# A cross-attention network on one core: layers unrolled, the next layer's keys and values inside a layer's last unit, normalisation through PSUM on ScalarE, MLP weight splits on ScalarE and VectorE

## What is computed

```python
# stage 0: grouped attention over the context, 32 heads of 16, 8 key heads, then residual and layer norm
x = layer_norm(x + softmax(q k^T / 4 + mask) v @ Wo + bo) * gamma + beta
# layers 0 and 1: cross attention, 16 heads of 128, one extra key and value (bias_k, bias_v) per head
for ly in (0, 1):
    h = layer_norm(x) * scale + offset
    x = x + softmax(concat(k, bias_k) . q / sqrt(128)) . concat(v, bias_v) @ wo + bo
# MLP of width 2048
h = layer_norm(x) * scale + offset
x = x + gelu(h @ w_fc1 + b_fc1) @ w_fc2 + b_fc2
```

## Time and profile before

| what | value |
|---|---|
| median of 3 runs | 2657.53 us (2656.21 to 2658.27) |
| profiled execution | 2658.52 us |
| its span, first to last instruction | 2656.7 us |
| mean granted clock of PE | 0.963 |
| PE busy | 2428.2 us, 91% |
| DVE, ACT, POOL busy | 1313.4, 791.8, 882.5 us |
| transfers | 120.09 MB, mean 45 GB/s |

### The profile page before, as it was taken

The page is one execution under the profiler, slowest core; times in us unless marked ns, Lnnn a source line. Parts: engine busy times, 40 slices in busy tenths (PEclk is TensorE's granted clock), DMA queues, the critical chain, the costliest instruction groups (busy, mean ns, idle before and its releaser), DMA issues.

```text
span 2656.7 us, 40799 instructions
## 1 busy us (share of the span) xinstructions
PE 2428.2 (91%) x14896; PEld 2076.7 (78%) x14896; DVE 1313.4 (49%) x2066; ACT 791.8 (30%) x2390; POOL 882.5 (33%) x568
## 2 busy tenths in 40 slices
PE   6867999998899999888977779999988999998888
PEld 5656888887788888667765568888877888886676
DVE  6976333344533343555479763334355334336444
ACT  5862222222222222211158522222222222222111
POOL 4853322232422232322157532223224223224221
PEclk9988999999999999999989889999999999999999
DMA  4001101010201010100130011011111011101000
GB/s 174 10 9 68 56 32 39 32 55 22 78 32 39 32 55 32 44 32 32 64 140 9 25 60 48 32 39 39 47 57 43 32 39 39 47 32 44 32 32 32
DMA packets 34534, 120.09 MB, mean 45 GB/s; under 512 B 3456, under 2 KB 3712, under 8 KB 33408
## 3 DMA queue, kind: packets, MB, share of 16 engines
q1 hardware_dynamic: 34432, 118.69, 12.7%
HBM read 114.48 MB, written 4.19 MB: 45 GB/s over the span
## 4 chain that ended last, share of the span: by engine, by line
PE 77%; DVE 8%; issue 6%; POOL 4%; ACT 3%; DMA 1%; SPq 0%; DVEq 0%; POOLq 0%; ACTq 0%
PE PS L453 64%; PE PS L664 4%; PE PS L646 4%; PE PS L655 2%; POOL X L319 1%; DVE X L1012 1%; DMA BO<-in_bo_rows 1%; PE PS L521 1%; PE PS L555 1%; DVE HF L1087 1%; DVE XN L988 1%; POOL W L306 1%; DVE BNS L1022 1%; DVE HB L1240 0%; DVE AT L1079 0%
## 5 line engine op out<-in xcount | busy, mean ns | idle before, releaser
L453 PE MATMUL PS<-AT,W 128*128 128x512 f32 x2496 | 609.2, 396 | 25.2 <-DVE HF L1087 12.1
L453 PEld LDWEIGHTS PS<-AT,W 128*128 128x128 f32 x2496 | 474.3, 191 | 129.9 <-issue 13.2
L1012 DVE TENSOR_TENSOR X<-PS,X 128x512 f32<-128x512 f32 x416 | 284.4, 690 | 333.1 <-PE PS L453 326.4
L394 POOL TENSOR_TENSOR PR<-PR,RC 128x512 f32<-128x512 f32 x128 | 133.5, 1043 | 932.1 <-DVE RC L1178 932.1
L453 PE MATMUL PS<-CT,W 128*128 128x512 f32 x1584 | 401.2, 403 | 28.8 <-DVE W L306 25.6
L453 PE MATMUL PS<-W,CT 128*128 128x256 f32 (+1 forms) x3264 | 410.3, 286 | 0.0
L453 PEld LDWEIGHTS PS<-W,CT 128*128 128x128 f32 x3264 | 399.6, 194 | 0.6
L453 PE MATMUL PS<-W,CX 128*128 128x512 f32 x1584 | 388.7, 399 | 11.8 <-DVE X L1012 8.6
L453 PEld LDWEIGHTS PS<-CT,W 128*128 128x128 f32 x1584 | 292.8, 192 | 86.7 <-DVE W L306 26.0
L453 PEld LDWEIGHTS PS<-W,CX 128*128 128x128 f32 x1584 | 292.9, 189 | 76.9 <-DVE X L1012 12.7
L313 POOL TENSOR_SCALAR W<-RAW 128x1024 fp32r<-128x1024 f32 (+1 forms) x136 | 154.6, 1137 | 546.5 <-PE PS L453 524.8
(11 more groups left out here) (102 smaller groups left out, 2531.9 us busy)
## 6 DMA issues: line engine op xcount, KB each, us to landing
RAW<-in_wq SPq DMA_DIRECT2D x44, 512.0 KB, 4.1
RAW<-in_wo SPq DMA_DIRECT2D x44, 512.0 KB, 3.3
RAW<-in_wk SPq DMA_DIRECT2D x40, 512.0 KB, 3.3
RAW<-in_wv SPq DMA_DIRECT2D x40, 512.0 KB, 3.3
X<-in_x SPq DMA_DIRECT2D x2, 2048.0 KB, 10.0
BVR<-in_bv_rows SPq DMA_DIRECT2D x8, 512.0 KB, 4.2
BIASVR<-in_biasv_rows SPq DMA_DIRECT2D x8, 512.0 KB, 5.6
out<-X SPq DMA_DIRECT2D x4, 1024.0 KB, 4.4
```

The lines of the kernel that those rows point to most:

```text
L394: nc.gpsimd.tensor_tensor(PR[:, :, 0:P], PR[:, :, 0:P], RC[:, 0, 0:BT].unsqueeze(2).to_broadcast([P, BT, P]), ALU.mult).then_inc(norm_done, 1)
L453: ins = nc.tensor.matmul(out, lhs(c, a), rhs(c, b), start=(k == 0), stop=(k == total - 1))
L1012: V_.tensor_tensor(X[:, tile, :], PS[:, bank, :], X[:, tile, :], ALU.add).then_inc(done, 1)
```

## The change

- The loop over the two layers is unrolled in the code of every engine (`for ly in range(LAYERS)`); the loop over `g` stays for the inner pairs.
- K has a buffer for each of the two heads.
- A layer's last unit is written out by hand. Towards layer 1 it holds keys and values of the next layer's first unit and the transposes of the normalised block 0; the rows of the last unit come as ordinary `rows`, and the next layer's first unit (`next_unit`) has no keys of its own. Towards the MLP it holds the transposes, parts of the last rows, and the first hidden block comes ahead of the rest of the last rows.
- Statistics are taken as rows are added (`add_block(..., measured=True)`).
- `to_at` is gone: ACT writes the scaled chunk as high part to AT and again, in place, to the PSUM bank; DVE subtracts from the bank (`lows`). `warm` is a one-element activation that loads a function table ahead of its use.
- In the MLP, PE's order is hidden m, down m-1 throughout, across pairs; ACT writes the high part of the slabs (`whi`), DVE the low part (`wlo`), POOL none but the first pair's v and o slabs.
- SP loads bias rows at two points inside the layer before; POOL subtracts and adds them inside the last and first units.

The diff, cut to its core:

```diff
-        K = in_arena("K", [P, BT, 132], F32, 2048)
+        K = in_arena("K", [P, 2, BT, 132], F32, 2048)
...
+                sp.wait_ge(v_ev, half_units(hf, 0) * 2 + NB1)
+                load_rows(1, 0)
+                with sp.Fori(G1 // 2 + 1, G1 + 1, 1) as g:
+                    load_slabs(g)
+                sp.wait_ge(v_ev, half_units(hf, 1) * 2)
+                load_rows(1, 1)
+                load_bo(2)
...
+                    even(G1 - 1)
+                    n = b0 + (NB1 - 1)
+                    weights(n, 0)
+                    if ly + 1 < LAYERS:
+                        sub_rows(ly + 1, 0)
+                    pool.wait_ge(q_ps, n * 2 + 2)
+                    psplit(0, lq + G1)
+                    if ly + 1 < LAYERS:
+                        psplit(2, lv + G1)
+                        weights(n, 1)
+                        add_layer_bo(ly + 1, 0)
+                        sub_rows(ly + 1, 1)
+                    else:
+                        weights(n, 1)
...
+                add_layer_bo(LAYERS, 0)
+                psplit(2, lv)
                 pool.wait_ge(o_ps, half_units(hf, LAYERS) * BT)
                 psplit(3, lq)
-                with pool.Fori(1, FG // 2, 1) as gp:
...
+                add_layer_bo(LAYERS, 1)
...
+                    def next_unit():
+                        queries(b0, 0, 0, lq, at_now)
+                        values(b0 + 1, 1, lv, -5, (0,))
+                        scores(b0, 0)
+                        queries(b0, 0, 1, lq)
+                        pe.wait_ge(q_ev, b0 * 2 + 2)
+                        pe.wait_ge(k_ev, b0 * 2 + 2)
+                        norm_t(norm_index(hf, ly), 1, BANKS_WARM)
+                        transposes(b0, 0)
+                        values(b0 + 1, 1, lv, -5, (1,))
+                        pe.wait_ge(at_lo, at_now + C + 1)
+                        weigh(b0, 0, 0)
+                        scores(b0, 1)
+                        pe.wait_ge(at_lo, at_now + 2 * C)
+                        keys(b0 + 1, 1, 0, lk)
+                        queries(b0 + 1, 1, 0, lq)
+                        transposes(b0, 1)
+                        values(b0 + 1, 1, lv, -5, (2, 3))
+                        weigh(b0, 0, 1)
+                    def last_unit_to_layer():
...
+                        scores(n, 1)
+                        keys(n + 1, 0, 0, lk + G1)
+                        values(n + 1, 0, lv + G1, -5, (0, 1))
+                        transposes(n, 1)
+                        pe.wait_ge(t_ev, n * 2 + 2)
+                        norm_t(norm_index(hf, ly + 1), 0, BANKS_NEXT)
+                        weigh(n, 1, 1)
+                        values(n + 1, 0, lv + G1, -5, (2, 3))
+                        rows(n, lq + g)
+                        keys(n + 1, 0, 1, lk + G1)
+                    def last_unit_to_mlp():
+                        g, n = G1 - 1, b0 + (NB1 - 1)
+                        scores(n, 0)
+                        keys(n, 1, 1, lk + g)
+                        rows(n - 1, lq + g)
+                        queries(n, 1, 1, lq + g)
+                        transposes(n, 0)
+                        scores(n, 1)
+                        weigh(n, 1, 0)
+                        norm_t(norm_index(hf, LAYERS), 0, BANKS_LAST, range(2))
+                        pe.wait_ge(cx_lo, n * 2 + 1)
+                        rows_part(0, 0)
+                        rows_part(1, 0)
+                        pe.wait_ge(exp_done, n * 2 + 2)
+                        norm_t(norm_index(hf, LAYERS), 0, BANKS_LAST, range(2, C))
+                        transposes(n, 1)
+                        weigh(n, 1, 1)
...
+                hidden(0, 0, True, (0,))
+                last_rows()
+                hidden(0, 0, True, (1,))
+                hidden(0, 1, True)
+                down(0, 0, True, range(2))
+                norm_t(norm_index(hf, LAYERS), 1, BANKS_MLP)
+                down(0, 0, True, range(2, BT))
+                down(0, 1, True)
+                hidden(0, 2, True)
+                hidden(0, 3, True)
+                down(0, 2, True)
+                with pe.Fori(1, FG // 2, 1) as gp:
+                    hidden(gp, 0)
+                    down(gp - 1, 3)
                     for m in range(1, 4):
+                        hidden(gp, m)
+                        down(gp, m - 1)
+                down(FG // 2 - 1, 3)
...
+                def norm_high(ly, tb, banks, chunks=range(C)):
+                    t, cols = norm_index(hf, ly) * TB + tb, layer_cols(ly)
+                    for c in chunks:
+                        act.wait_ge(tr_ps, t * C + (c + 1))
+                        for dst, done in ((AT[:, 0, c, tb * BTOK:(tb + 1) * BTOK], at_hi), (PS[:, banks[c], :], f_done)):
+                            nc.scalar.activation(dst, PS[:, banks[c], :], ACT.Identity, ...).then_inc(done, 1)
...
+                def whi(n, count, done):
+                    act.wait_ge(ld[n], count * 16 + 16)
+                    act.wait_ge(*done)
                     take_wait(act)
+                    nc.scalar.activation(W[:, n, 0, :], RAW[:, n, :], ACT.Copy).then_inc(w_hi[n], 1)
...
+                        if first and m == 0:
+                            root((hf + 1) * 8 - 1)
+                            warm(ACT.Gelu)
                         if first and m == 1:
+                            norm_high(LAYERS, 1, BANKS_MLP)
+                        if m < 2 and not first:
+                            whi(2 + m, (lv, lq)[m] + gp, (m_ps, m0 * BT - (1 - m) * BT))
+                        if m >= 2 and not last:
+                            whi(m - 2, (lq, lv)[m - 2] + gp + 1, (h_ps, m0 * 2 + 2 * m + 2))
...
+                def lows(i, tb, banks, chunks=range(C)):
+                    t = i * TB + tb
+                    for c in chunks:
+                        dve.wait_ge(f_done, t * C + (c + 1))
+                        V_.tensor_tensor(AT[:, 1, c, tb * BTOK:(tb + 1) * BTOK], PS[:, banks[c], :],
                                          AT[:, 0, c, tb * BTOK:(tb + 1) * BTOK].bitcast(F32), ALU.subtract).then_inc(at_lo, 1)
...
+                        add_block(n - 1, 0, True)
+                        cx_low(n, g, 0)
+                        top(n, 1)
+                        variances(rounds + 2, 1e-5)
+                        inverse(n, 1)
+                        roots(rounds + 2)
+                        dve.wait_ge(tr_ps, i * TB * C)
+                        apply(0)
+                        kev(n + 1, 0, 0, layer_cols(ly + 1))
+                        vev(n + 1, 0, 0, (0,), ly + 1)
+                        lows(i, 0, BANKS_NEXT, range(2))
+                        cx_low(n, g, 1)
+                        lows(i, 0, BANKS_NEXT, range(2, C))
+                        vev(n + 1, 0, 0, (1,))
...
+                def first_pair():
...
+                    stats(1, range(BT), x_count(hf, n) + 1)
+                    variances((hf + 1) * 8 - 1, 1e-5)
+                    hsplit(0, 0)
+                    roots((hf + 1) * 8 - 1)
                     apply(1)
+                    hsplit(0, 1)
+                    madd_(0, 0, True, range(2))
...
+                def pair(gp, last=False):
+                    hsplit(gp, 0)
+                    madd_(gp - 1, 3)
+                    wlo(2, lv + gp)
                     for m in range(1, 4):
+                        hsplit(gp, m)
+                        madd_(gp, m - 1)
+                        if m == 1:
+                            wlo(3, lq + gp)
+                        elif not last:
+                            wlo(m - 2, (lq, lv)[m - 2] + gp + 1)
```

More of the change, by code:

```diff
@@ L248, in load_half @@
                 load_slabs(0)
[L249 to L262, removed]
@@ new lines, in values @@
+                def values(n, tb, slab, adds, parts=range(4)):
+                    w = W[:, 2].rearrange("p a (c n) -> p a c n", n=256)
+                    for p in parts:
+                        i, b = p // 2, p % 2
+                        if p == 0:
+                            pe.wait_ge(w_ready[2], slab + 1)
+                        if b == 0 and adds is not None:
+                            pe.wait_ge(xadd, x_count(hf, n) + (i + adds))
+                        t = (tb * BT + p) * P
+                        ins = triple(PS[:, BC + i, b * 256:(b + 1) * 256], lambda c, a: CT[:, a, c, t:t + P],
+                                     lambda c, b_: w[:, b_, c, :], C)
+                        if b:
+                            ins.then_inc(v_ps, 1)
@@ new lines, in hidden @@
+                def hidden(gp, m, first=False, blocks=range(2)):
+                    e, tb, m0 = m % 2, m // 2, hf * FG * TB + gp * 4
+                    pe.wait_ge(w_ready[e], (lv if e else lq) + gp + 1)
+                    for f in blocks:
+                        if m or not first:
+                            pe.wait_ge(gelu_done, m0 * 2 + (2 * m + f - 1))
+                        fresh = mlp_now + tb * C if first and e == 0 and f == 0 else None
```

(27 more changed lines are left out.)

764 lines of the change are left out of this document (417 added, 347 removed).

## The result

The changed kernel takes 2571.51 us (median of 4 runs, 2567.79 to 2574.21) against 2657.08 for the kernel before on the same chip: ratio 0.9677, 95% interval 0.966 to 0.9693, so 85.6 us faster; 78 was forecast. Its profiled execution took 2574.21 us (span 2572.4, mean granted clock 0.975 for 0.963).

The account below looks back on a forecast made before the run. TensorE, busy 2428 of 2657 us, bounds the kernel; only waits and the clock lost with them can be won. 12.2 + 11.3 + 11.9 + 3.7 = 39.1 per half, 78 in all: 2658.5 - 78 = 2580 us, range 2550 to 2612.

Parts of the forecast that it names:

- Pairs 1 and 2 are pair 3 without POOL: MLP loop: with POOL's slab work gone, pairs 1 and 2 each take pair 3's 44.96 us; 12.2 us won per half.
- MLP change: Layer 1 to MLP with its first pair: waits 12.6 instead of 21.3 us, clock 5.7; 11.9 us won per half.
- Layer change, four waits and one "at most": Layer 0 to 1: waits 1.6, 1.3, 1.0, 2.6 and at most 1.0, sum 7.5 instead of 15.0; 11.3 us won per half.
- 0.44 carried over: At both changes: each us of TensorE waiting costs another 0.42 to 0.47 us through the clock.
- The in-place write: Normalisation: ACT's write to PSUM taken as 0.69 us, between 0.35 and 1.4; at 1.4, 8.4 us per half at most.
- Table loads at 1.28 and 0.2: ACT at both changes: a table switch costs 1.28 us and the one-element activation some 0.2, against the skill's 2.66.
- Steady units, "nothing won or lost": Steady units inside the layers: same instructions in the same order, so 0 us won or lost.
- Normalisation path: Low parts read PSUM, free of POOL's blocking; priced separately only in layer 0's first unit, 3.7 us won per half.
- Rival 1: Less gain: DVE's twelve low parts per half land before row additions, costing 30 us in all, 2610 us; chance 0.17.
- Rival 2: More gain: waits too short and scattered to pull the clock, BO's addition misses the HB subtraction; 2554 us, chance 0.17.
- Rival 3: Slower: small waits spread over the changes lower the clock; with 45% of that work slowed, 2693 us; chance 0.04.
- Rival 4: Nothing won: ACT's in-order slab waits and refetched code eat the gain, 3.7 us per moved slab; 2657 us, chance 0.03.

Follow-up runs that it names:

- experiment 1: The kernel before with only the MLP's weight slabs split on ACT (high part) and DVE (low part) instead of POOL: 2621.9 us, ratio 0.9863.
- experiment 2: The changed kernel with the MLP's weight slabs split on POOL again, all else as changed: 2604.67 us, ratio 0.9795.
- Experiment 3: The kernel before with only the short normalisation path: ACT scales the PSUM bank in place, DVE subtracts from it: 2626.82 us, ratio 0.9886.
- 6c: The kernel before with an unused 4-byte tensor ahead of the arena, moving it and CX by 32 bytes: 2657.45 us, ratio 1.0001.
- 6d: The changed kernel with all layer-stage buffers, CX included, at the addresses of the kernel before: 2564.45 us, ratio 0.9649.

## Why the prediction was right

It came to 2580 with 2550 to 2612; measured 2571.5. By its steps:

- *Pairs 1 and 2 are pair 3 without POOL.* All three take 44.95 us at clock 1.00, 12.3 won for 12.2. Right, and shown by experiments 1 and 2 from both sides. In experiment 1 the third stretch wins 19.1, as the first pair has the two waits as well; the forecast had that in the MLP change.
- *Layer change, four waits and one "at most".* 1.22, 0.95, 0.94 and 2.37 for 1.6, 1.3, 1.0 and 2.6. The fifth, queries behind root and the Exp load, did not come: no load stands ahead of the root (below), and the queries follow one load. Sum 5.5 for 7.5. PE busy 59.81 over the 56.6 of pure work is 3.2 for the 3.3 given to the clock; as the waits are smaller, that is 0.58 of them and not the 0.44 carried over.

ACT of the changed kernel there, in order of time:

```profile
667.68 0.21 ACT L933 ACTIVATE SD<-NT 128x4 f32<-128x4 f32 x1 [9.99 <-DVE NT L1210]
667.90 1.28 ACT L972 ACT_TABLE_LOAD   x1
...
669.31 0.67 ACT L983 ACTIVATE Q<-PS,BQS 128x512 f32<-128x512 f32 x1
```

- *MLP change: the term that was mis-sized most.* 83.3 us for 87.5. Waits 2.75, 1.46, 1.67, 0.82, 0, 3.02 for 2.8, 1.1, 2.8, 1.2, 0.5, 4.2, so 9.7 for 12.6. The places hold. The subtraction blocked by BO's addition took 4.94 us, as in the earlier trace rows, so what was off at the last wait is only where PE met it. PT did stand behind a Gelu load and two chunks, as the forecast has it (ACT from 1088.84 to 1093.50), but PE ran out of work only at 1091.88. The smaller misses at chunk 3 and the rows stay unexplained. The clock took 73.51 - 69.2 = 4.3, 0.44 of the waits, the ratio that was carried over.
- *The in-place write* was taken as 0.69 between 0.35 and 1.4. It is 754 ns to PSUM and 777 to SBUF, starting 0.66 apart:

```profile
L967 ACT ACTIVATE AT<-PS,VEC x48: 759/777/814, 204.2 to 2398.2; 128x512 fp32r<-128x512 f32 x48
L967 ACT ACTIVATE PS<-PS,VEC x48: 739/754/790, 204.8 to 2398.8; 128x512 f32<-128x512 f32 x48
```

- *Table loads at 1.28 and 0.2.* Two loads back to back at the MLP change:

```profile
1080.91 1.28 ACT L933 ACT_TABLE_LOAD   x1 [7.82 <-DVE NT L1210]
1082.21 0.20 ACT L933 ACTIVATE SD<-NT 128x4 f32<-128x4 f32 x1
1082.43 1.28 ACT L972 ACT_TABLE_LOAD   x1
```

The next load starts 1.52 us behind the first. The Trainium skill, ScalarE: Activation LUTs, What ACT_TABLE_LOAD costs, gives 2.66 us a switch with a drain of 1.38; no such drain stands here, and the measurement decides.

- *Steady units, "nothing won or lost": the step that failed.* It named the same instructions in the same order as its reason, which held; that an operand's address has a price it did not consider. It cost 8 us in all. The stretches with waits won some 16 us more than forecast, 8 of them at the MLP changes, so the sum is off by only 8: that it came so near is in part luck.
- *Normalisation path.* The forecast put its gain into the stretches and gave it no price of its own except in the first unit of layer 0, by blocked subtractions: 3.7 for 4.5, of which the path alone wins 3.9. Experiment 3 shows that the same holds at the layer change, where the wait of 2.53 in the kernel before stood behind such subtractions too, and that at the change to the MLP the earlier start of ACT counts for more. The Trainium skill, GPSIMD Engine Reference, Specifications (contention with VectorE instructions with two SBUF inputs) agrees: its VectorE instructions with two SBUF inputs are the ones seen blocked here, and the 48 low parts that read PSUM stay at 678 to 693 ns in the changed kernel.
- *Rivals.* Rival 1 needed late additions: none in 90 us of pairs. Rival 2 had the size (2554), not the reason: the clock still takes 0.44 and more of each wait and BO's addition did hit the subtraction. Rival 3 would show as a low clock in the changes; it is 0.97 and 0.96, up from 0.91. Rival 4 would leave the time at 2657, and no wait of PE in the pairs is left for ACT's high parts to cause; its price per slab was off as well, since 78 over 24 slabs is 3.25 and not 3.7.

Open: which property of its address makes CX slow. Only the address before (of four tried) is fast. 6c keeps every distance inside the arena and has the slow rows, so the distance from CX to another buffer of the arena is not it; the four don't separate the alignment of the address from the distance to a buffer outside the arena, such as W. Nor is the wider scatter explained: the change's four runs spread over 6.4 us, the four of 6d over 3.3.

## What to carry to other kernels

Look for VectorE operations that take 2 to 5 us for 0.69 beside GpSimd before counting the links of a chain, and move such an operation's input to PSUM or its neighbour off GpSimd: that was the gain of the split and of the path at the layer change. A shorter chain wins by itself where VectorE is late with its first link, as at the change to the MLP. Cost a moved addition by what it will lie beside, and make it wait for that. When buffers move, compare a steady stretch with its twin before, and undo all parts of a displacement at once: half of it undone proves nothing.

## What the runs showed that was not expected

- The pace of matmuls depends on where the stationary operand lies in SBUF: 24 of them take 5.57 us with CX at one address and 5.67 to 5.69 at three others, 32 to 2144 bytes further (232 ns and 236 to 237 each), while the weight loads show 187 to 188 ns in all.
- POOL's hold on DVE does not depend on the size of DVE's operation. In the changed kernel, four numbers per partition with two SBUF inputs took 2.29 us, on the path to the roots, and ended with POOL's subtraction at 1085.14:

```profile
1082.79 2.35 POOL L324 TENSOR_TENSOR W<-RAW,W 128x1024 fp32r<-128x1024 f32 x1
1082.85 2.29 DVE L1217 TENSOR_TENSOR NS<-NT,RS 128x4 f32<-128x4 f32 x1
```

Its neighbour of the same shape took 0.16 ahead of it.
